# An eight-stage transformer kernel on one core: recurrence started on three takes, waits per norm chunk, a direct last reciprocal, bias rows laid out, a root table loaded at the start

## The chip, the cores and the metric

One core of one Trainium2 chip. The time is device microseconds of one launch; the kernel before has three timed runs, and one more run that the profiler recorded. Lines written as L12 are lines of the kernel before.

## The reference

The input x is one sequence of 2048 tokens of width 128, in f32. Eight blocks follow, each with its residual, `x = x + f(layernorm(x))`:

1. an RWKV-6 recurrence: projections r, k, v, w of token-mixed inputs, per head (16 of width 8) `s = exp(w)*s + k v^T`, output `r (s + exp(u+k) v^T)`, a norm per head, the gate r and an output matrix;
2. a mixture of 8 experts with the two best gates (hidden width 256);
3. causal attention with rotation, 16 heads of width 8;
4. the mixture of step 2 again, with the same weights;
5. full attention with one head of width 128;
6. a mixture of 8 experts that takes only two distinct sets of weights (expert 0, and a perturbed copy shared by the other seven), hidden width 512, with an inner norm that feeds its router;
7. causal attention with low-rank keys and values, 8 query heads, 2 key heads;
8. the mixture of step 6 again.

```
s = jnp.exp(w_t)[..., None] * s + k_t[..., :, None] * v_t[..., None, :]
...
h = (x - mu) * jax.lax.rsqrt(var + 1e-05) * ln_gamma + ln_beta
probs = jax.nn.softmax(logits, axis=-1)
out = jnp.einsum('bse,besh->bsh', probs, y)
```

## The kernel before

x (`X`), its norm (`H`) and the transposed norm (`HT`, features on partitions) stay in SBUF. The 2048 tokens are 16 tiles of 128, or NC = 4 chunks of 512 (TPC = 4 tiles each). Every stage is a class with one method per engine (`sync`, `gpsimd`, `tensor`, `scalar`, `vector`), and each engine runs the methods of all stages in their order, so its instructions run in exactly the order that the code writes. Semaphores alone hold the engines together; DMAs of the stages are issued from SP.

**LayerNorm** (L191 on). VectorE makes statistics, ScalarE takes the root of the variance (L298, or L249 for one chunk), VectorE takes the reciprocal (L280) and normalises (L283, L234), TensorE transposes a chunk into a PSUM bank (L242), and ScalarE copies it to `HT` (L259), which raises `ready` by one per chunk. A norm behind a mixture or the recurrence has chunks 0 to 2 done while the stage before it still runs; behind an attention all four are made at its start. The banks are 0 to 3. The next stage's TensorE waits for `all_ready`, all four chunks.

**Rwkv** (L708 on). For each chunk of 512 tokens ScalarE *takes* six results (`take`): k, w, r and v out of four PSUM banks, w scaled, and `ek = exp(u+k)`. VectorE then computes `rk = r*ek` (L838), and for each of 8 state columns j: the outer product `kvj` (L789) from TensorE's repeated values (`values`, L958), the recurrence as one scan (L844), and `rsj = r*state` (L861), which TensorE sums over j into bank 6 (L1008). TensorE sums rk over heads (L998) into bank 0, ahead of its loop over j, and VectorE multiplies that with v (`bonus`, L800) at j = 1. The next chunk's projections (L946, L947) are issued at j = 5. VectorE adds both parts at the chunk's end (`output`, L794), and TensorE centres the sum and takes its variance (L966, L971) at the start of the next chunk.

**Experts** (L1029 on). For each chunk and expert: `hidden` (L1065), gelu on ScalarE (L1118), `output`: a 3-row matmul that puts the bias rows in the bank (L1076, its moving operand the expert's row of 128 read four times through a step of 0), then L1083, and VectorE's gated addition to x (L1148). In the first chunk the router (L1191, then a chain of small VectorE operations from L1205) comes behind `hidden` of expert 1; in the two mixtures of the second kind the inner norm stands ahead of it.

**CausalHeads** (L1240 on), used twice, as `rope` and `latent`. A prologue projects `HT` (L1441, L1443), projects the values (L1449), splits the results in three bf16 parts and writes and rereads them through DRAM by SP. `make_plan` then writes out an order for scores, exponentials, weighted sums and a ring of small items in PSUM banks 5 to 7. For `latent` the sums of a chunk of queries are one item `total` (L1505); they are copied to SBUF (L1766), moved by a DMA into a 128x16 tile, inverted (L1705), moved back by a DMA, spread over the partitions by a matmul (item `sum`, L1498), multiplied with O (L1761), and multiplied with the output weights (item `out`, L1512; then L1772).

**FullHead** projects q, k, v (L1977, L1982), and then goes tile by tile. `Perturb` runs on GpSimd alongside stages 2 to 5 and delivers the second set of weights of stage 6; its bias rows are split by VectorE in eight small steps that end with L578.

## Time and profile before

| | |
|---|---|
| median of 3 runs | 1744.61 us (1743.3 to 1746.62) |
| the profiled execution | 1749.35 us |
| its span | 1747.3 us |
| mean granted TensorE clock in it | 0.935 of full |
| TensorE busy | 1561.8 us (89%) |
| VectorE busy | 1071.8 us (61%) |
| ScalarE busy | 793.4 us (45%) |
| GpSimd busy | 748.2 us (43%) |

All rows come from the one profiled execution, which took 4.7 us more than the median of the other runs. Starts are microseconds from the span's start. A group of matmuls in f32 counts each multiplication twice (two passes). A row's bracket names the idle time of its engine ahead of it and what ended it.

### The profile page before, as it was taken

To read this page: it belongs to the slowest core of one execution; us is meant where nothing else is said; L and a number is where in the kernel's file an instruction comes from. 1 tells how busy PE (TensorE), PEld (TensorE's weight loads), DVE (VectorE), ACT (ScalarE), POOL (GpSimd) and SP (SyncE) were. 2 spreads that over 40 slices of the span, in tenths; PEclk is the share of its full clock that TensorE was granted. 3 is DMA by queue.
4 is the path that set the end of the run, shared out by engine and by line. 5 is a ranking of instruction groups with operands and counts; after the bars stand their busy time and mean duration, and the time that the engine had idled before them with its cause. 6 is when DMAs were issued, how large, how long until landed. Compare 5 with 4: busy or idle time off the path is not lost.

```text
span 1747.3 us, 25466 instructions
## 1 busy us (share of the span) xinstructions
PE 1561.8 (89%) x8943; PEld 803.1 (46%) x8943; DVE 1071.8 (61%) x2338; ACT 793.4 (45%) x1037; POOL 748.2 (43%) x963
## 2 busy tenths in 40 slices
PE   5886999689999999999799979997978799999789
PEld 2433666323343333343266647775744343343256
DVE  5777433798788788786143333334348889885541
ACT  2231444615555555556534424445452334445442
POOL 1000663654635455463645546360002457777600
PEclk9998899859999999999889989998988899999879
DMA  5000000323002011000000000000034100000000
GB/s 154 0 1 1 1 1 1 121 54 56 2 2 56 2 28 30 2 2 3 1 1 1 1 1 0 0 0 1 1 99 131 40 24 2 2 1 2 1 7 19
DMA packets 41353, 37.18 MB, mean 21 GB/s; under 512 B 12404, under 2 KB 38493, under 8 KB 41117
## 3 DMA queue, kind: packets, MB, share of 16 engines
q1 hardware_dynamic: 38948, 28.61, 5.8%
q10 hardware_dynamic: 2136, 7.10, 2.1%
q8 instruction: 70, 1.15, 0.3%
q14 instruction: 39, 0.31, 0.1%
q0 software_dynamic: 160, 0.01, 0.0%
HBM read 26.09 MB, written 8.91 MB: 20 GB/s over the span
## 4 chain that ended last, share of the span: by engine, by line
PE 70%; DVE 13%; ACT 3%; issue 3%; DMA 1%; POOL 1%; SPq 1%; DVEq 0%; POOLq 0%; ACTq 0%
PE PS L1539 11%; PE PS L1083 10%; PE PS L1481 10%; PE PS L1558 10%; PE PS L1065 9%; PE PS L1993 3%; PE PS L2011 3%; DVE sb_rope_mp L1728 3%; DVE sb_latent_mp L1728 2%; PE PS L2005 1%; PE PS L1498 1%; PE PS L1076 1%; POOL sb_H L1649 1%; PE PS L1512 1%; PE PS L1191 1%
## 5 line engine op out<-in xcount | busy, mean ns | idle before, releaser
L1728 DVE TENSOR_REDUCE sb_rope_mp<-PS 128x1 f32<-128x512 f32 (+3 forms) x560 | 344.6, 668 | 68.7 <-PE PS L1485 31.9
L1600 ACT ACTIVATE sb_rope_PT<-PS 128x1024 f32<-128x1024 f32 (+3 forms) x320 | 273.4, 895 | 210.5 <-PE PS L1543 109.4
L1148 DVE SCALAR_TENSOR_TENSOR sb_X<-PS,sb_gates,sb_X 128x128 f32<-128x128 f32 x320 | 90.1, 344 | 225.7 <-PE PS L1083 225.3
L1481 PE MATMUL PS<-sb_rope_K,sb_rope_Q 96*128 96x512 bf16 (+3 forms) x640 | 213.6, 373 | 11.5 <-ACT sb_rope_V L1585 7.9
L643 POOL TENSOR_SCALAR sb_pbelow<-sb_pa,sb_ptrial 128x512 f32<-128x512 f32 x124 | 194.7, 1581 | 6.4
L1728 DVE TENSOR_REDUCE sb_latent_mp<-PS 128x1 f32<-128x512 f32 (+2 forms) x280 | 176.0, 668 | 26.8 <-PE PS L1481 15.8
L650 POOL TENSOR_TENSOR sb_pbelow<-sb_pbelow 128x1024 f32<-128x1024 f32 (+1 forms) x248 | 181.4, 731 | 19.6
L1065 PE MATMUL PS<-sb_HT,sb_w 128*128 128x512 f32 x384 | 182.7, 613 | 4.3 <-DVE sb_seed L578 1.9
L1539 PE MATMUL PS<-sb_rope_Q,sb_rope_K 99*128 99x512 bf16 (+3 forms) x640 | 180.2, 353 | 1.6 <-ACT sb_rope_PT L1600 0.9
L1558 PE MATMUL PS<-sb_rope_PT,sb_rope_V 128*9 128x512 f32 (+3 forms) x1280 | 149.8, 540 | 0.1
L1539 PE MATMUL PS<-sb_latent_Q,sb_latent_K 96*128 96x512 bf16 (+7 forms) x640 | 149.7, 353 | 0.0
L1118 ACT ACTIVATE sb_moe_hidden<-PS,sb_vec 128x512 f32<-128x512 f32 x128 | 86.7, 687 | 130.4 <-PE PS L1065 124.4
L1481 PEld LDWEIGHTS PS<-sb_rope_K,sb_rope_Q 96*128 96x128 bf16 x640 | 59.8, 100 | 167.8 <-issue 82.2
L1083 PE MATMUL PS<-sb_w0b,sb_moe_hidden 128*128 128x128 f32 x1024 | 133.7, 285 | 0.0
L1083 PEld LDWEIGHTS PS<-sb_w0b,sb_moe_hidden 128*128 128x128 f32 x1024 | 121.3, 194 | 14.7 <-issue 14.7
L1481 PE MATMUL PS<-sb_latent_K,sb_latent_Q 96*128 96x512 bf16 (+3 forms) x320 | 102.3, 369 | 12.7 <-DVE sb_latent_mp L1728 6.0
L1065 PEld LDWEIGHTS PS<-sb_HT,sb_w 128*128 128x128 f32 x384 | 70.8, 198 | 71.2 <-issue 66.7
L656 POOL TENSOR_TENSOR sb_ptot<-sb_ptot,sb_prank 128x8 f32<-128x8 f32 x31 | 6.2, 200 | 221.3 <-issue 221.3
L655 POOL PARTITION_ALL_REDUCE sb_ptot<-sb_pcnt x31 | 13.3, 427 | 185.3 <-issue 185.3
L1539 PEld LDWEIGHTS PS<-sb_rope_Q,sb_rope_K 99*128 99x128 bf16 x640 | 59.0, 99 | 69.5 <-issue 17.1
L1539 PEld LDWEIGHTS PS<-sb_latent_Q,sb_latent_K 99*128 99x128 bf16 (+1 forms) x640 | 57.1, 99 | 72.7 <-issue 17.0
L1543 PE MATMUL PS<-sb_mask_kq,sb_identb 128*128 128x128 bf16 x384 | 81.2, 226 | 0.0
(330 smaller groups left out, 2496.4 us busy)
## 6 DMA issues: line engine op xcount, KB each, us to landing
sb_latent_Q<-latent_parts SPq DMA_DIRECT2D x48, 128.0 KB, 2.7
sb_rope_Q<-rope_parts ACTq DMA_DIRECT2D x9, 384.0 KB
rope_parts<-sb_rope_parts SPq DMA_DIRECT2D x24, 128.0 KB, 2.4
latent_parts<-sb_latent_parts SPq DMA_DIRECT2D x12, 256.0 KB, 2.5
sb_rope_tab<-in_rotation SPq DMA_DIRECT2D x1, 2048.0 KB, 7.8
sb_rope_K<-rope_parts ACTq DMA_DIRECT2D x6, 256.0 KB
latent_parts<-sb_latent_parts SPq DMA_DIRECT2D x12, 128.0 KB, 2.5
sb_latent_K<-latent_parts SPq DMA_DIRECT2D x48, 32.0 KB, 2.2
```

What stands on the lines that cost most here:

```text
L643: ch.mark(g.tensor_scalar(self.below[:, w, s, :], self.a[:, w, :], tr[:, 2 * w + s:2 * w + s + 1], None, ALU.is_lt))
L650: ch(g.tensor_tensor(bl[:, :, 0:n], bl[:, :, 0:n], bl[:, :, n:2 * n], ALU.add))
L1065: pe.matmul(k.bank(b), self.w1(e, m), x, start=True, stop=True).then_inc(self.hid[b], 1)
L1083: ins = pe.matmul(k.PS[:, 4 + b, i * P:(i + 1) * P], self.g[:, b, m, i * P:(i + 1) * P], self.w2(e, m), start=False, stop=(m == M - 1), sk ...
L1118: s.activation(self.g[:, e % 2, m, :], k.bank(b), self.func, bias=self.b1(e, m)) \
L1148: ins = v.scalar_tensor_tensor(xi, k.PS[:, 4 + b:5 + b, i * P:(i + 1) * P], gate, xi, ALU.mult, ALU.add)
L1481: ins = pe.matmul(k.PS[:, bank, at:at + w], self.Q[0:self.rows, g % 2, j, 0, q0:q0 + P], self.K[0:self.rows, g % 2, j % self.kheads, 0, kc ...
L1539: ins = pe.matmul(k.PS[:, j, q0:CH], self.K[0:r, g % 2, j % self.kheads, m, kj * P:(kj + 1) * P], self.Q[0:r, g % 2, j, m, c * CH + q0:(c ...
L1543: ins = pe.matmul(k.PS[:, j, q0:q0 + P], k.identb[:, :], k.mask_kq[:, :], start=False, stop=True)
L1558: ins = pe.matmul(k.PS[32 * j:32 * j + self.vcols, 4, q0:CH], v, self.PT[u % self.B][:, j, q0:CH], start=(kj == 0), stop=(kj == last))
L1600: s.activation(self.PT[u % self.B][:, 2 * p:2 * p + 2, q0:CH], k.PS[:, 2 * p:2 * p + 2, q0:CH], ACT.Exp, scale=self.scale).then_inc(self.e ...
L1728: ins = v.tensor_reduce(self.mp[:, n % 2, kc, heads[0]:heads[-1] + 1, i], k.PS[:, bank, 0:len(heads) * w].rearrange("p (h k) -> p h k", h= ...
```

## The change

It has seven parts.

1. *Table at the start.* `Setup.scalar` takes the root of a column of constants, ahead of everything else on ScalarE; `sd` is overwritten by the first norm later.
2. *Three takes.* The order of the projections and takes is w, k, r, v (was k, w, r, v), w is scaled right behind the take of k, and VectorE starts a chunk's first outer product after three takes. The first `rsj` waits for the fourth, `rk` stands behind the outer product of j = 1 and waits for all six.
3. *Bonus two steps on.* TensorE's matmul on rk moves from the head of the chunk to behind the sum of j = 1, VectorE's `bonus` from j = 1 to j = 3.
4. *Waits per chunk.* TensorE waits for chunk c of the norm only where it projects chunk c, in the mixtures and in both causal stages; the router, the inner norm and the value projections wait for all. In the full attention the wait for all stays ahead of the first projection. Every norm but the first transposes into banks 4 to 7.
5. *Bias rows.* Per mixture a tile `seeds` holds the rows four times over, written by four DMAs from SP, which waits for the norm's statistics (and for the rows themselves); the moving operand of L1076 is then contiguous.
6. *Direct last reciprocal.* The last chunk of the last causal stage has an item `direct` in the place of `total`, both DMAs, the 128x16 reciprocal and `sum`: VectorE inverts each 128x128 quarter of the PSUM bank in place and multiplies O with it, and `out` starts on each quarter as it is ready.
7. One new semaphore per mixture, and the counts and waits that go with these parts.

```
--- before.py
+++ after.py
     def scalar(self, s):
         s.wait_ge(self.zeroed, self.n_zeroed)
+        s.activation(self.k.ln_mem.sd[:, 0:1], self.k.eps[:, :], ACT.Sqrt).then_inc(self.pool, 1)
+        s.wait_ge(self.pool, 1)
...
-            v.wait_ge(self.taken, (c + 1) * self.TAKEN)
-            if c:
-                v.wait_ge(self.bonus, c)
-            v.tensor_tensor(self.rk[:, :], self.r[:, c % 2, :], self.ek[:, :], ALU.mult).then_inc(self.rk_ready, 1)
+            v.wait_ge(self.taken, c * self.TAKEN + 3)
             outer(c, 0)
...
                 if j == 1:
+                    v.wait_ge(self.taken, (c + 1) * self.TAKEN)
+                    if c:
+                        v.wait_ge(self.bonus, c)
+                    v.tensor_tensor(self.rk[:, :], self.r[:, c % 2, :], self.ek[:, :], ALU.mult) \
+                        .then_inc(self.rk_ready, 1)
+                if j == 3:
                     bonus(c)
...
+                if j == 0:
+                    v.wait_ge(self.taken, c * self.TAKEN + 4)
...
-            plain = [(self.kk, 1, ACT.Copy), (self.w, 3, ACT.Sigmoid), (self.r, 0, ACT.Sigmoid), (self.v, 2, ACT.Copy)]
+            plain = [(self.w, 3, ACT.Sigmoid), (self.kk, 1, ACT.Copy), (self.r, 0, ACT.Sigmoid), (self.v, 2, ACT.Copy)]
...
-            s.wait_ge(self.taken, c * self.TAKEN + 2)
-            s.activation(self.w[:, p, :], self.w[:, p, :], ACT.Copy, scale=float(np.exp(-1e-4))).then_inc(self.taken, 1)
+                if i == 1:
+                    s.wait_ge(self.taken, c * self.TAKEN + 1)
+                    s.activation(self.w[:, p, :], self.w[:, p, :], ACT.Copy, scale=float(np.exp(-1e-4))) \
+                        .then_inc(self.taken, 1)
...
-            for n, bank in ((1, 1), (2, 3), (0, 0)):
+            for n, bank in ((2, 3), (1, 1), (0, 0)):
...
-            pe.wait_ge(self.rk_ready, c + 1)
-            pe.matmul(k.bank(0), k.group_sum, self.rk[:, :], start=True, stop=True).then_inc(self.bonus, 1)
             for j in range(8):
...
+                if j == 1:
+                    pe.wait_ge(self.rk_ready, c + 1)
+                    pe.matmul(k.bank(0), k.group_sum, self.rk[:, :], start=True, stop=True).then_inc(self.bonus, 1)
...
+        self.seeds = self.k.sb(self.name + "_seeds", [3, self.E, TPC, P], BF16, ctx)
+
+    def sync(self, sp):
+        for sem, val in self.needs:
+            sp.wait_ge(sem, val)
+        sp.wait_ge(self.ln.mem.moments, self.ln.all_ready)
+        for i in range(TPC):
+            sp.dma_start(self.seeds[:, :, i, :], self.seed[:, :, :]).then_inc(self.seeded, 16)
...
-        pe.wait_ge(self.ln.ready, self.ln.all_ready)
         def turn(c, first):
+            pe.wait_ge(self.ln.ready, self.ln.chunk_ready(c))
...
-                pe.matmul(k.bank(4 + b), k.onesb[0:3, :],
-                          self.seed[:, e:e + 1, :].broadcast_to([3, TPC, P]), start=True, stop=False,
+                if c == 0 and e == 0:
+                    pe.wait_ge(self.seeded, self.seeded_at)
+                pe.matmul(k.bank(4 + b), k.onesb[0:3, :], self.seeds[:, e, :, :], start=True, stop=False,
...
-            if first:
+            if first and self.between:
+                pe.wait_ge(self.ln.ready, self.ln.all_ready)
...
+                if n == len(self.order) - 1:
+                    steps[end + 2] += [("direct", g, c), ("out", g, c)]
+                    continue
...
-        pe.wait_ge(self.ln.ready, self.ln.all_ready)
         for c in range(NC):
+            pe.wait_ge(self.ln.ready, self.ln.chunk_ready(c))
...
                 pe.wait_ge(self.filled, self.use + 1)
+                pe.wait_ge(self.ln.ready, self.ln.all_ready)
...
-        pe.wait_ge(self.normed, n + 1)
         for i in range(TPC):
+            pe.wait_ge(self.normed, n + 1 + (i if ("direct", g, c) in self.ring_items() else 0))
...
+        elif kind == "direct":
+            n = self.chunk(*item[1:])
+            v.wait_ge(self.moved, n + 1)
+            for i in range(TPC):
+                tile = slice(i * P, (i + 1) * P)
+                ch(v.reciprocal(k.PS[:, bank, tile], k.PS[:, bank, tile]))
+                ch(v.tensor_tensor(self.On[:, n % 2, tile], self.O[:, n % 2, tile], k.PS[:, bank, tile], ALU.mult))
+                v.sem_inc(self.normed, 1)
+            v.sem_inc(free, 1)
...
-            ln = LayerNorm(k, k.X, k.H, k.HT, x_ready)
+            ln = LayerNorm(k, k.X, k.H, k.HT, x_ready, banks=(4, 5, 6, 7) if len(stages) > 1 else (0, 1, 2, 3))
```

The change moves instructions in the recurrence. On VectorE, at the start of the first chunk, these rows stood before (rw_rk is r times ek, rw_kvj the outer product, the operation on rw_state the scan, rw_rsj the state times r, rw_o the bonus):

```order
L838 TENSOR_TENSOR sb_rw_rk<-sb_rw_r,sb_rw_ek 128x512 [waits rwkv_taken]
L789 TENSOR_TENSOR sb_rw_kvj<-sb_rw_k,PS 128x512 [waits rwkv_vrep0]
L844 SCALAR_TENSOR_TENSOR sb_rw_state<-sb_rw_w,sb_rw_state,sb_rw_kvj 128x512 [waits rwkv_kv0,rwkv_steps]
L789 TENSOR_TENSOR sb_rw_kvj<-sb_rw_k,PS 128x512 [waits rwkv_vrep1]
L861 TENSOR_TENSOR sb_rw_rsj<-sb_rw_r,sb_rw_state 128x512 [waits rwkv_kv_used0]
L844 SCALAR_TENSOR_TENSOR sb_rw_state<-sb_rw_w,sb_rw_state,sb_rw_kvj 128x512 [waits rwkv_kv1]
L789 TENSOR_TENSOR sb_rw_kvj<-sb_rw_k,PS 128x512 [waits rwkv_kv_used0,rwkv_vrep0]
L800 TENSOR_TENSOR sb_rw_o<-PS,sb_rw_v 128x512 [waits rwkv_bonus]
L861 TENSOR_TENSOR sb_rw_rsj<-sb_rw_r,sb_rw_state 128x512 [waits rwkv_kv_used1]
```

Now, in the same place:

```order
L793 TENSOR_TENSOR sb_rw_kvj<-sb_rw_k,PS 128x512 [waits rwkv_vrep0,rwkv_taken]
L845 SCALAR_TENSOR_TENSOR sb_rw_state<-sb_rw_w,sb_rw_state,sb_rw_kvj 128x512 [waits rwkv_kv0,rwkv_steps]
L793 TENSOR_TENSOR sb_rw_kvj<-sb_rw_k,PS 128x512 [waits rwkv_vrep1]
L870 TENSOR_TENSOR sb_rw_rsj<-sb_rw_r,sb_rw_state 128x512 [waits rwkv_taken,rwkv_kv_used0]
L845 SCALAR_TENSOR_TENSOR sb_rw_state<-sb_rw_w,sb_rw_state,sb_rw_kvj 128x512 [waits rwkv_kv1]
L793 TENSOR_TENSOR sb_rw_kvj<-sb_rw_k,PS 128x512 [waits rwkv_kv_used0,rwkv_vrep0]
L853 TENSOR_TENSOR sb_rw_rk<-sb_rw_r,sb_rw_ek 128x512 [waits rwkv_taken]
L870 TENSOR_TENSOR sb_rw_rsj<-sb_rw_r,sb_rw_state 128x512 [waits rwkv_kv_used1]
```

The product rk went from ahead of the first outer product to behind the third, into the place where the bonus stood; the bonus itself is two steps further on.

On TensorE, in the same chunk, before (rw_mixv to wvrep is the repeated value, rw_rk the head sum of the bonus, rw_rsj the output sum):

```order
L958 MATMUL PS<-sb_rw_mixv,sb_wvrep 128x512 [waits setup_ready]
L958 MATMUL PS<-sb_rw_mixv,sb_wvrep 128x512
L998 MATMUL PS<-sb_rw_rk,sb_cst 128x512 [waits rwkv_rk_ready]
L958 MATMUL PS<-sb_rw_mixv,sb_wvrep 128x512 [waits rwkv_kv0]
L1008 MATMUL PS<-sb_rw_rsj,sb_cst 128x512 [waits rwkv_rs0]
```

and now:

```order
L969 MATMUL PS<-sb_rw_mixv,sb_wvrep 128x512 [waits setup_ready]
L969 MATMUL PS<-sb_rw_mixv,sb_wvrep 128x512
L969 MATMUL PS<-sb_rw_mixv,sb_wvrep 128x512 [waits rwkv_kv0]
L1017 MATMUL PS<-sb_rw_rsj,sb_cst 128x512 [waits rwkv_rs0]
L969 MATMUL PS<-sb_rw_mixv,sb_wvrep 128x512 [waits rwkv_kv1]
L1017 MATMUL PS<-sb_rw_rsj,sb_cst 128x512 [waits rwkv_rs1]
L1021 MATMUL PS<-sb_rw_rk,sb_cst 128x512 [waits rwkv_rk_ready]
```

The third repeated value no longer stands behind the head sum. The same moves are made in all four chunks.

## Rows read from the trace of the kernel before

**Rows 1.** The profile's page: busy time by engine, and the chain's shares.

```profile
PE 1561.8 (89%) x8943; PEld 803.1 (46%) x8943; DVE 1071.8 (61%) x2338; ACT 793.4 (45%) x1037; POOL 748.2 (43%) x963
...
PE 70%; DVE 13%; ACT 3%; issue 3%; DMA 1%; POOL 1%; SPq 1%; DVEq 0%; POOLq 0%; ACTq 0%
```

**Rows 2.** Timeline of the start: start us, duration us, engine, line, instruction, count.

```profile
11.85 1.28 ACT L298 ACT_TABLE_LOAD   x1 [11.85 <-DVE sb_mv L277]
...
20.78 2.04 PE L946 MATMUL PS<-sb_HT,sb_wmix 128*128 128x512 f32 x2 [1.58 <-DVE sb_wvrep L459]
```

**Rows 3.** Timeline, first chunk of the recurrence.

```profile
29.90 1.88 PE L958 MATMUL PS<-sb_rw_mixv,sb_wvrep 128*128 128x512 f32 x4
...
33.24 0.90 DVE L838 TENSOR_TENSOR sb_rw_rk<-sb_rw_r,sb_rw_ek 128x512 f32<-128x512 f32 x1 [9.35 <-ACT sb_rw_ek L898]
34.07 0.67 DVE L789 TENSOR_TENSOR sb_rw_kvj<-sb_rw_k,PS 128x512 f32<-128x512 f32 x1
```

**Rows 4.** Timeline, second, third and fourth chunk of the recurrence.

```profile
62.33 0.68 DVE L838 TENSOR_TENSOR sb_rw_rk<-sb_rw_r,sb_rw_ek 128x512 f32<-128x512 f32 x1
62.93 0.68 DVE L789 TENSOR_TENSOR sb_rw_kvj<-sb_rw_k,PS 128x512 f32<-128x512 f32 x1
...
68.05 2.06 PE L998 MATMUL PS<-sb_rw_rk,sb_cst 128*128 128x512 f32 x2
...
69.89 1.71 PE L958 MATMUL PS<-sb_rw_mixv,sb_wvrep 128*128 128x512 f32 x2
...
71.64 0.69 DVE L789 TENSOR_TENSOR sb_rw_kvj<-sb_rw_k,PS 128x512 f32<-128x512 f32 x1 [4.26 <-PE PS L958]
...
101.30 1.40 PE L998 MATMUL PS<-sb_rw_rk,sb_cst 128*128 128x512 f32 x2
...
104.45 0.69 DVE L789 TENSOR_TENSOR sb_rw_kvj<-sb_rw_k,PS 128x512 f32<-128x512 f32 x1 [1.37 <-PE PS L958]
...
134.12 1.10 PE L998 MATMUL PS<-sb_rw_rk,sb_cst 128*128 128x512 f32 x2
...
136.12 0.69 DVE L789 TENSOR_TENSOR sb_rw_kvj<-sb_rw_k,PS 128x512 f32<-128x512 f32 x1 [0.23 <-PE PS L958]
```

**Rows 5.** Timeline, where stages 2, 3 and 6 begin.

```profile
170.28 1.11 PE L242 MATMUL PS<-sb_cst,sb_H 128*128 128x128 f32 x4 [3.90 <-DVE sb_H L234]
...
172.13 6.13 PE L1065 MATMUL PS<-sb_HT,sb_w 128*128 128x512 f32 x8 [0.73 <-issue]
...
322.17 0.69 DVE L1676 TENSOR_TENSOR sb_rope_x<-PS,sb_rope_tab 128x512 f32<-128x512 f32 x1 [3.63 <-DMA sb_rope_tab<-in_rotation]
...
1204.92 8.60 PE L1065 MATMUL PS<-sb_HT,sb_w 128*128 128x512 f32 x16 [1.92 <-DVE sb_seed L578]
```

**Rows 6.** Stretch of 1 us: busy per engine, then PEclk, DMA share, GB/s.

```profile
172.00:173.00 1.00, 0.87 (x1) 0.50 (x2) 0.00 (x0) 0.03 (x1) 0.57 (x6) 0.50 0.00 0
```

**Rows 7.** Timeline of TensorE, full clock, in stage 2 and in stage 3.

```profile
229.22 0.38 PE L1076 MATMUL PS<-sb_seed,sb_onesb 3*128 3x512 bf16 x1
229.53 2.05 PE L1083 MATMUL PS<-sb_w0b,sb_moe_hidden 128*128 128x128 f32 x16
...
564.74 0.38 PE L1481 MATMUL PS<-sb_rope_K,sb_rope_Q 96*128 96x512 bf16 x1
565.05 1.05 PE L1558 MATMUL PS<-sb_rope_PT,sb_rope_V 128*9 128x512 f32 x8
```

**Rows 8.** Timeline, end of stage 7, with one reciprocal and one product from elsewhere.

```profile
75.53 0.55 DVE L807 RECIPROCAL sb_rw_sd<-sb_rw_sd 128x64 f32<-128x64 f32 x1
...
182.78 0.29 DVE L1205 TENSOR_TENSOR sb_rt_p<-PS,sb_bg 128x128 f32<-128x128 f32 x1 [12.55 <-PE PS L1191]
...
1647.03 1.93 PE L1505 MATMUL PS<-sb_H,sb_cst 128*32 128x512 f32 x8 [3.54 <-POOL sb_H L1649]
...
1651.66 0.25 DVE L1705 RECIPROCAL sb_latent_inv<-sb_latent_sums 128x16 f32<-128x16 f32 x1 [1.95 <-DMA sb_latent_sums<-sb_latent_x]
...
1658.92 0.69 DVE L1772 TENSOR_TENSOR sb_X<-sb_X,PS 128x512 f32<-128x512 f32 x1 [2.29 <-PE PS L1512]
```

9 lines of the change are left out of this document (7 added, 2 removed).

## The prediction, made before the changed kernel was run

> **What bounds the kernel now.** I read the page first: TensorE is busy 89% of the span and holds 70% of the chain that ended last, VectorE 13% [rows 1]. So an edit pays only where TensorE stands idle, or where VectorE holds the chain: the start, the head of each chunk of the recurrence, the seams between stages and the tail of stage 7. I then read the timeline at each of those places, TensorE and VectorE side by side; in every row the bracket says how long the engine had stood still and who ended that. A row without a bracket follows its forerunner directly. Last I looked at the granted clock where TensorE had just been idle, because a matmul there takes about twice its time [rows 4, 6].
>
> The sum is made against the profiled execution, 1749.35 us, 4.7 above the median of the runs. I take off the gains there and then those 4.7.
>
> **Table at the start.** ScalarE loads the root table for 1.28 us after VectorE's statistics are there [rows 2]; the normalised x waits for that root, and TensorE's first projection waits on VectorE behind it, with 1.58 idle [rows 2]. The new root on a constant column makes the load before the statistics, while ScalarE waits anyway. Gain 1.28 at most, 0 at least if the chain through L459 were set by other VectorE work; I take **-1.3**, since the load stands between two links of that chain.
>
> **Three takes, first chunk.** VectorE began with rk at 33.24, released by ek, the last of the takes after 9.35 idle, and the outer product followed at 34.07 [rows 3]. The outer product now needs k, w and the first repeated value. The four passes of the two repeated values start at 29.90 and take 1.88, 0.47 each [rows 3], so the first value is there at about 30.9. That is 3.1 earlier. The product rk isn't gone: it moves behind the third outer product and costs its slot there, 0.60 from its start to the next one's [rows 4]. Something of the rest is lost where the first rsj waits for the fourth take. 3.1 - 0.6 = 2.5 is the upper bound; a lower one is 1.9, if rsj waits 0.6; I take **-2.2**. The table of the sigmoid is also loaded behind the first projection now and not ahead; that lies beside the four passes of k's projection, and nobody waits for it.
>
> **The other three chunks.** The head sum L998 stood ahead of the third repeated value on TensorE, and VectorE waited for that value: 4.26, 1.37 and 0.23 in chunks two to four [rows 4]. In chunk two L998 takes 2.06 and its successor starts 1.84 later; in chunk three it takes 1.40, in chunk four 1.10 [rows 4]. It leaves this place (its new one, behind the sum of j = 1, is where TensorE waits for VectorE), and the wait shrinks by its slot. VectorE pays 0.60 for rk behind the outer product, as it did ahead of the first, where it was hidden in the wait. So: chunk two -1.84 + 0.6 = -1.2; chunk three about -1.2 + 0.6 = -0.6; in chunk four only 0.23 of wait and the freed 0.6 ahead can be won, some -0.2. Together **-2.0**, from 0 (the projections of the next chunk simply absorb it) to -3. The bonus two steps later has the same length in the same stream: 0. What is late next in these places is the repeated value itself, 1.71 for its two passes at the low clock [rows 4].
>
> **Waits per chunk.** In stage 2 the last transposes end, TensorE stands 0.73 for ScalarE's copy, and the first `hidden` begins [rows 5]. Chunk 0 has long been copied, so the new wait is met: TensorE can go on behind its transposes, at most 0.95 early, which is the copy and the hand-over (170.28 + 1.11 to 172.13 is 0.74; the ends of matmuls are modelled, and a wait that doesn't exist saves its own latency too, about 0.2). But the granted clock stands at 0.50 there [rows 6], the 1.2 GHz level, after TensorE had waited 3.90 for VectorE [rows 5]. If the clock rises at the same instant as before and not earlier, the early microsecond is worked at half speed and half of the gain is gone: 0.45. I take 0.7, and four such seams (stages 2, 4, 7 and 8): **-2.8**. In stage 3 the same wait goes, but VectorE's first product waits until 322.17 for the DMA that brings the rotation table [rows 5], which nobody moves: 0 to -0.9, I take **-0.4**. In stage 6 TensorE waits for L578 on VectorE, 1.92 [rows 5], and not for the norm: 0. In the full attention the wait for all stays: 0. The router and inner norm still wait for all, but they come two `hidden` later, when all chunks are there. Other banks for the transposes take a possible wait for `hidden`'s banks away: 0, since the first group of the next stage uses banks that are free. Together **-3.2**, bounds 0 and -5.
>
> **Bias rows laid out.** The matmul with the repeated row holds TensorE for 0.31 from its start to the next one's, its record is 0.38. A bf16 matmul over 512 columns with a contiguous operand, in the scores of stage 3, shows 0.31 and 0.38 as well ahead of an f32 matmul [rows 7]. So the step of 0 costs nothing that could be won: **0**. The rows' DMAs (four per mixture, on SP) start at the norm's statistics and are wanted behind the first two `hidden`, at least 10 us later: hidden. If that cover were gone, TensorE would stand by what is missing of a transfer.
> The Trainium skill, "TensorE: Matmul & The Clock Gate", section Back-to-back issue gap, gives about 216 ns for an isolated warm matmul of N=512; by that the slot of 0.31 would hide 0.1 of something, and with 80 such matmuls the sum would have 7.5 more to win. The neighbouring row speaks against it.
>
> **Direct last reciprocal.** Now, from the sums' matmul on: start 1647.03, 1.93 long, copy, DMA out, 0.25 of reciprocal at 1651.66, DMA back, `sum`, product, `out`; VectorE's addition starts at 1658.92 after 2.29 for L1512 [rows 8]. In its place come four times a reciprocal of 128x128 and a product. No row has this reciprocal. The nearest are 128x64 with 0.55 and 128x16 with 0.25 [rows 8], both in SBUF: a slope of 0.30/48 = 6.25 ns per element of a partition gives 0.95. Lower bound 0.55 (no longer than half of it), upper bound 2 (PSUM in place at twice the slope); I take 0.95, along the line through both rows. The product takes 0.29 [rows 8], the hand-over some 0.06: 1.3 per quarter, 5.2 for four, from 1649.0 to 1654.2. TensorE's `out` on quarters one to three runs underneath; the last needs about 0.5. VectorE then adds at 1654.7, not 1658.92: **-4.2**. With 0.55 it would be -5.8, with 2 a quarter it is 0.
> By the Trainium skill, "VectorE: DVE Perf Modes", section First, the fixed hardware budget, a reciprocal is divided iteratively with a repeat count of 8; at the 0.96 GHz of its Specifications that is 8.3 ns per element, by my estimate 1.2 a quarter and -3.2 for the part. The step between the two rows is somewhat smaller than this rule's.
>
> **Sum.** -1.3 - 2.2 - 2.0 - 3.2 - 4.2 = -12.9: 1736.4 for a profiled execution like the one shown, **1731.7** for the median.
>
> **The rivals.**
> *Other waits take the place of the norm's.* For: stage 3 does it already, by the table's DMA, and the clock is at its low level at the seam [rows 5, 6]. Against: in stages 2, 4, 7 and 8 nothing else is late. Then -3.2 goes: 1734.9. Chance 0.14.
> *The reciprocal in PSUM is slow.* For: no row has one from PSUM. Against: the product with a PSUM operand takes 0.29 for 128 columns, nothing unusual [rows 8]. At 2 a quarter the part gives 0: 1735.9. From there on it would lose. Chance 0.08.
> *The repeated row is what costs the bias matmul.* For: 0.38 is long for 512 columns at full clock. Against: the contiguous row of the same group [rows 7]. Worth 0.1 x 80 = 7.5 to 8: 1724. Chance 0.07.
> *The clock is lost in the recurrence: slower.* TensorE there runs at both levels; a pass costs 1.71 / 2 = 0.86 at the low one and 1.88 / 4 = 0.47 at the full one [rows 3, 4]. The head sum filled TensorE for 1 to 2 us at each chunk's start. With it gone from there, and VectorE's stream longer by rk at j = 1, TensorE has a longer idle stretch, and the granted clock may fall and stay low over the 16 passes of the next chunk's projections: 16 x 0.39 = 6.2 at each of three seams. One seam gives 1737.9; two 1744.1, no change; all three 1750.3, slower. It decides when the third falls. Against it: chunk two runs low already at the head without its projections having been lost, and the passes only change place. One seam 0.02 (it counts to faster), two 0.02, three 0.03.
> *It doesn't do what it says,* since each removed wait was met before: the starts stay where they are, 1744.6. The brackets speak against it. Chance 0.02.
>
> **How the numbers follow.** The forecast has the rest, 0.64. Its own bounds: the direct part from 0.55 to 1.3 a reciprocal, +1.4 and -1.6; recurrence +2 and -1; seams +3.2 and -1.8; table +1.3; these don't fall together, and each low-clock stretch may shift, by some 1.7 us, as the 2.06 against 1.10 of the head sum shows. The runs themselves lie within 3.3. I give **1725.5 to 1738.0**: it reaches from just above the bias-row rival to one seam of lost clock, and leaves out some 0.15 to 0.2. About 3.5 us, 0.2%, is what a measurement of this kernel can tell from no change. Faster: the forecast, the first three rivals, one seam lost: 0.95, less 0.02 for a forecast that meets several bounds at once: 0.93. Same, two seams, a change that does nothing, and nothing more: 0.04. Slower: 0.03.
>
> **What would show it.** Right: the load of the root table before the statistics; the first outer product near 29.7, released by the repeated value; no head sum between the second and third repeated value; in stage 2 the first `hidden` within about 0.2 of the transposes; four reciprocals of about 0.95 in the last chunk, and VectorE's last addition 4 us sooner; the bias matmul's slot still at 0.31. Wrong: reciprocals of 2 us or more, a granted clock of 0.5 over the projections inside the recurrence, or TensorE waiting for the rows' DMAs in a first chunk.

## The result, and the profile after

The changed kernel takes 1731.08 us (median of 6 runs, 1722.39 to 1733.3) against 1745.47 of the kernel before (6 runs, 1743.3 to 1746.86): ratio 0.9913, with a 95% interval of 0.9897 to 0.993, so 14.4 us faster. 1731.7 was forecast. Lines are those of the changed kernel from here on, unless it says "before".

The profiled execution, though, took 1722.39 us: 27 below that of before, not 14. A single profile of this kernel stands several us off its median, as the runs below show. The page's first part and the chain's shares answer to [rows 1]:

```profile
PE 1546.3 (90%) x8941; PEld 799.8 (46%) x8941; DVE 1076.7 (63%) x2343; ACT 793.2 (46%) x1038; POOL 748.2 (43%) x963
...
PE 71%; DVE 13%; ACT 3%; issue 3%; POOL 1%; DMA 1%; SPq 1%; DVEq 0%; POOLq 0%; ACTq 0%
```

TensorE is busy 15.5 us less with the same matmuls but one (the last chunk's `sum`, two passes, 2.05 us before). The rest is the clock: a wait taken away can't shorten a matmul. To see where, I cut both traces at the first matmul of each part: the first `hidden` of stages 2, 4, 6 and 8, the first projection and the first score of stages 3 and 7. The view gives busy time per engine in each stretch, then the granted clock, the DMA share and GB/s. Before:

```profile
0.00:172.10 172.10, 124.75 (x367) 58.75 (x367) 124.35 (x262) 45.84 (x71) 6.22 (x21) 0.95 0.14 39
172.10:317.90 145.80, 140.40 (x720) 91.93 (x720) 55.17 (x205) 59.85 (x83) 83.72 (x137) 0.94 0.02 6
317.90:350.70 32.80, 21.57 (x64) 10.29 (x64) 26.86 (x40) 26.76 (x28) 18.27 (x27) 0.86 0.48 145
350.70:880.20 529.50, 490.31 (x3265) 188.61 (x3265) 397.95 (x755) 285.46 (x343) 270.74 (x453) 0.93 0.10 19
880.20:1204.90 324.70, 301.93 (x1680) 209.03 (x1680) 120.48 (x334) 137.04 (x206) 154.44 (x247) 0.96 0.00 1
1204.90:1285.40 80.50, 73.62 (x392) 52.36 (x392) 29.75 (x141) 41.85 (x58) 0.00 (x0) 0.92 0.00 1
1285.40:1309.50 24.10, 16.60 (x57) 8.63 (x58) 14.81 (x24) 16.06 (x32) 0.00 (x0) 0.85 0.57 172
1309.50:1670.00 360.50, 321.31 (x2025) 132.24 (x2025) 283.97 (x499) 150.69 (x175) 214.77 (x80) 0.92 0.09 25
```

After:

```profile
0.00:162.20 162.20, 119.84 (x368) 58.11 (x369) 124.33 (x262) 45.10 (x71) 7.04 (x21) 0.95 0.14 42
162.20:305.40 143.20, 137.62 (x721) 89.87 (x721) 57.78 (x205) 59.63 (x83) 81.08 (x134) 0.96 0.02 5
305.40:337.50 32.10, 21.34 (x66) 10.46 (x64) 26.30 (x41) 27.26 (x29) 17.49 (x26) 0.87 0.51 152
337.50:858.10 520.60, 486.02 (x3265) 187.95 (x3265) 396.04 (x754) 284.80 (x342) 268.25 (x447) 0.94 0.09 20
858.10:1182.60 324.50, 302.40 (x1681) 209.14 (x1680) 120.21 (x333) 137.81 (x207) 160.02 (x258) 0.96 0.00 1
1182.60:1262.30 79.70, 73.54 (x392) 52.53 (x393) 29.76 (x141) 41.29 (x56) 0.00 (x0) 0.93 0.00 1
1262.30:1285.10 22.80, 15.34 (x58) 8.21 (x56) 14.75 (x24) 16.70 (x33) 0.00 (x0) 0.87 0.59 181
1285.10:1643.30 358.20, 318.90 (x2023) 132.29 (x2024) 288.54 (x501) 150.11 (x174) 214.28 (x80) 0.93 0.09 25
```

The first stretch gives 9.9, the last one shown 2.3, and those with the seams around stages 2, 3 and 7 together 5 to 6; behind it, stage 8 takes 77.3 in both. The fourth, 8.9, is the main part of stage 3, in which the change touches nothing but the seam at its end, where stage 4 begins.

At the chosen places, the timeline (start us, duration us, engine, line, instruction) answers to [rows 2] and [rows 3] like this:

```profile
11.86 0.31 ACT L300 ACTIVATE sb_sd<-sb_mv,sb_eps 128x16 f32<-128x16 f32 x1 [9.63 <-DVE sb_mv L279]
...
19.49 1.10 PE L957 MATMUL PS<-sb_HT,sb_wmix 128*128 128x512 f32 x2 [1.30 <-DVE sb_wvrep L463]
...
25.57 3.00 PE L969 MATMUL PS<-sb_rw_mixv,sb_wvrep 128*128 128x512 f32 x6
...
26.70 0.69 DVE L793 TENSOR_TENSOR sb_rw_kvj<-sb_rw_k,PS 128x512 f32<-128x512 f32 x1 [4.11 <-PE PS L969]
```

The root follows the statistics with no load between, the first projection comes 1.3 earlier, and the outer product is released by TensorE and no longer by ek. But the projection takes 1.10 for two passes and not 2.04: here the clock had come up before it, in the trace of before only at 26.9. So the outer product starts 7.4 earlier, where 1.3 + 3.1 had been worked out.

Stage 2's seam and VectorE's first product of stage 3 answer to [rows 5], stage 7's tail to [rows 8]:

```profile
161.26 1.11 PE L244 MATMUL PS<-sb_cst,sb_H 128*128 128x128 f32 x4 [3.89 <-DVE sb_H L236]
162.17 5.13 PE L1087 MATMUL PS<-sb_HT,sb_w 128*128 128x512 f32 x8
162.41 0.60 ACT L261 ACTIVATE sb_HT<-PS 128x512 f32<-128x512 f32 x1 [2.57 <-PE PS L244]
...
310.11 0.69 DVE L1704 TENSOR_TENSOR sb_rope_x<-PS,sb_rope_tab 128x512 f32<-128x512 f32 x1 [3.17 <-DMA sb_rope_tab<-in_rotation]
```

```profile
1626.59 0.97 DVE L1797 RECIPROCAL PS<-PS 128x128 f32<-128x128 f32 x1 [2.67 <-PE PS L1533]
1627.59 0.29 DVE L1798 TENSOR_TENSOR sb_latent_On<-sb_latent_O,PS 128x128 f32<-128x128 f32 x1
1628.02 0.97 DVE L1797 RECIPROCAL PS<-PS 128x128 f32<-128x128 f32 x1
...
1633.12 0.69 DVE L1809 TENSOR_TENSOR sb_X<-sb_X,PS 128x512 f32<-128x512 f32 x1 [0.95 <-PE PS L1540]
```

The first `hidden` starts 0.91 behind the transposes' start, before 1.85, while ScalarE still copies the last chunk; the table's DMA still ends VectorE's wait; a reciprocal takes 0.97 and a quarter 1.43. At stage 4 the same wait of 0.73 is gone, first before, then after:

```profile
880.18 4.10 PE L1065 MATMUL PS<-sb_HT,sb_w 128*128 128x512 f32 x5 [0.73 <-issue]
```

```profile
857.19 1.12 PE L244 MATMUL PS<-sb_cst,sb_H 128*128 128x128 f32 x4 [0.46 <-DVE sb_H L285]
858.10 4.47 PE L1087 MATMUL PS<-sb_HT,sb_w 128*128 128x512 f32 x6
```

The bias matmul with the contiguous row keeps its slot of 0.31 (221.31 to 221.62) and its record [rows 7]:

```profile
221.31 0.39 PE L1100 MATMUL PS<-sb_moe_seeds,sb_onesb 3*128 3x512 bf16 x1
221.62 1.05 PE L1106 MATMUL PS<-sb_w0b,sb_moe_hidden 128*128 128x128 f32 x7
```

### The profile page after: what moved, and what is told of

It reads as the page before. It is cut to its first block, busy times and chain, and to the rows that moved or that the text cites. A ratio compares the mean times of both kernels' runs of the same rounds, so it can differ in the third digit from the quotient of the medians.

```text
span 1720.6 us, 25513 instructions
## 1 busy us (share of the span) xinstructions
PE 1546.3 (90%) x8941; PEld 799.8 (46%) x8941; DVE 1076.7 (63%) x2343; ACT 793.2 (46%) x1038; POOL 748.2 (43%) x963
## 4 chain that ended last, share of the span: by engine, by line
PE 71%; DVE 13%; ACT 3%; issue 3%; POOL 1%; DMA 1%; SPq 1%; DVEq 0%; POOLq 0%; ACTq 0%
PE PS L1567 11%; PE PS L1106 11%; PE PS L1509 10%; PE PS L1586 10%; PE PS L1087 10%; PE PS L2031 3%; PE PS L2049 3%; DVE sb_rope_mp L1756 3%; DVE sb_latent_mp L1756 2%; PE PS L2043 1%; PE PS L1100 1%; POOL sb_H L1677 1%; PE PS L1526 1%; PE PS L1540 1%; PE PS L1513 1%
## 5 line engine op out<-in xcount | busy, mean ns | idle before, releaser
L1509 PE MATMUL PS<-sb_latent_K,sb_latent_Q 96*128 96x512 bf16 (+3 forms) x320 | 101.4, 367 | 14.8 <-DVE sb_latent_mp L1756 8.3
L1513 PE MATMUL PS<-sb_mask_qk,sb_identb 128*128 128x128 bf16 x384 | 81.0, 236 | 0.0
```

The costliest lines, as they stand in the source:

```text
L1509: ins = pe.matmul(k.PS[:, bank, at:at + w], self.Q[0:self.rows, g % 2, j, 0, q0:q0 + P], self.K[0:self.rows, g % 2, j % self.kheads, 0, kc ...
L1513: ins = pe.matmul(k.PS[:, bank, at + w - P:at + w], k.identb[:, :], k.mask_qk[:, :], start=False, stop=True)
```

## The experiments

Twelve kernels ran, each beside runs of the kernel before on the same chip. Those 88 runs of before have a mean of 1746.5, a median of 1745.9, and lie between 1734.97 and 1760.84. Each run has its span and its mean granted clock, and with the two levels that gives the time at the lower one, 2 x (1 - clock) x span: 230 us on average for before. Among these 88 runs of one program, a run with 1 us more at the low level is 0.41 us longer (correlation 0.84). Most of the spread goes with that. For kernels that ran 12 times the mean has a standard error of 0.9 to 1.7 us, for 6 to 8 times 1.2 to 3.1, and a +- is one such error; I use medians and intervals as measured, and means where parts are added up.

### One part alone, on the kernel before

Part 1 alone:

```
         s.wait_ge(self.zeroed, self.n_zeroed)
+        s.activation(self.k.ln_mem.sd[:, 0:1], self.k.eps[:, :], ACT.Sqrt).then_inc(self.pool, 1)
+        s.wait_ge(self.pool, 1)
```

> The kernel before with part 1 alone (the root of a constant column at the start). Theory of waits: the load of 1.28 goes from between the statistics and the root, and nothing else, 1.3 us faster than before. Theory of the clock: the profile of the changed kernel has its first repeated value at 25.57 where before has it at 29.90, 4.3 earlier, because its first projections run 1.02 per pair of passes and not 2.04; if the earlier load is what brings the clock up sooner, this kernel alone is 3 to 4.5 us faster and its first projection takes 1.1 and not 2.04. If the moment at which the clock rises is a matter of chance, the runs of this kernel spread over some 3 us and the median stands near -1.3 to -2.5.

Measured: median 1742.52, ratio 0.9978 (0.9956 to 1.0), mean -3.6 against all runs of before. In the profile the first repeated value comes at 27.2 and the first `hidden` at 169.9; in three traces with an unchanged start they come at 28.4 to 29.9 and 171.1 to 172.1. The projection took 2.05 at first and full clock came at 22.9; the unchanged starts have it between 24 and 27. So 1.3 is the load. The clock's rise differs by up to 3 us between unchanged starts, and one trace at 22.9 doesn't tell whether the earlier load moves it.

Parts 2 and 3 alone:

```
-            v.wait_ge(self.taken, (c + 1) * self.TAKEN)
...
-            v.tensor_tensor(self.rk[:, :], self.r[:, c % 2, :], self.ek[:, :], ALU.mult).then_inc(self.rk_ready, 1)
+            v.wait_ge(self.taken, c * self.TAKEN + 3)
             outer(c, 0)
```

> The kernel before with part 2 and 3 alone (three takes, rk behind the outer product of j = 1, bonus at j = 3). Theory of waits, as predicted: -4.2 (first chunk -2.2, chunks two to four -2.0). Theory that the prediction undersized it: the span from the first repeated value to the first hidden of stage 2 was 142.2 in the profile of before and is 136.6 in that of the changed kernel, so -5.6. Clock theory: the difference beyond 4.2 comes from low stretches at another place, and then this run shows pairs of passes of 1.7 to 2.06 at other places than before and a median anywhere from -2 to -8.

Measured: median 1738.35, ratio 0.9955 (0.9936 to 0.9973), mean -7.6. The first `hidden` comes at 167.8, 3.8 below the mean 171.6 of the three unchanged ones: the prediction's 4.2. For the rest of the 7.6, 3.8, there is the time at the low level, 221 us a run against 230, which at 0.41 is 3.5; that is a match of two numbers and not shown to be the cause.

Part 4 alone:

```
-        pe.wait_ge(self.ln.ready, self.ln.all_ready)
         def turn(c, first):
+            pe.wait_ge(self.ln.ready, self.ln.chunk_ready(c))
```

> The kernel before with part 4 alone (waits per chunk, banks 4 to 7). Theory of waits: -3.2 (0.7 at stages 2, 4, 7 and 8, 0.4 at stage 3). Rival, other waits take the place: 0. Clock theory: the 27 us between the two profiles are only 14 between the medians, and 9 of them lie in stage 3's main part, where the low stretch shrank from 44 to 31 us; if the earlier start by the copy's wait moves such stretches, this kernel's runs spread by 5 us or more and its median can lie 5 or more below before.

Measured: median 1743.68, ratio 0.9966 (0.9942 to 0.999), mean -5.7. The runs fall apart in five at 1730 to 1737 and seven at 1744 to 1749, with 217 us at the low level. By stages: stage 7 starts 0.8 earlier behind stage 6 and its prologue takes 22.8 and not 24.1. The rows of stage 7's prologue show why, before and then after: four passes in 3.78, and in 2.88.

```profile
1285.41 3.78 PE L1441 MATMUL PS<-sb_HT,sb_wc 128*128 128x512 f32 x4 [0.69 <-ACT sb_HT L259]
```

```profile
1262.34 2.88 PE L1468 MATMUL PS<-sb_HT,sb_wc 128*128 128x512 f32 x4
1265.05 1.02 PE L1468 MATMUL PS<-sb_HT,sb_wkv 128*128 128x512 f32 x2
```

TensorE reached full clock sooner, where the prediction feared that the clock would stay put. Stage 7's main part took 1.1 of it back. Together 1.1 for the two seams of stages 7 and 8, and 1.2 up to stage 3's first projection. At stage 4, 0.94 comes on top: from the start of the last four transposes to the first `hidden` it is 1.85 at stages 2 and 4 in all six traces without the part and 0.91 in all eight with it.

Part 6 alone:

```
+                if n == len(self.order) - 1:
+                    steps[end + 2] += [("direct", g, c), ("out", g, c)]
+                    continue
```

> The kernel before with part 6 alone (direct last reciprocal). Predicted -4.2 at 0.95 per reciprocal and 1.3 per quarter. The changed kernel's profile shows 0.97 per reciprocal and 1.43 per quarter, and from the sums' matmul to the last addition 8.5 instead of 11.9: by that -3.4. Nothing ahead of stage 7's tail may differ; if the median is off by more than 1.5 from -3.4, the runs' own spread is larger than their median tells.

Measured: median 1742.78, ratio 0.9973 (0.9951 to 0.9996), mean -4.5. Stage 7's main part takes 357.0 and not 360.5: -3.5, as the rows of the tail give.

Part 5 alone:

```
-                          self.seed[:, e:e + 1, :].broadcast_to([3, TPC, P]), start=True, stop=False,
+                pe.matmul(k.bank(4 + b), k.onesb[0:3, :], self.seeds[:, e, :, :], start=True, stop=False,
```

> The kernel before with part 5 alone (bias rows laid out four times by DMAs). Theory as predicted: 0, and the bias matmul's slot still 0.31. Rival, the repeated row is what costs: 80 times 0.1, -7.5 to -8, with a slot of 0.22; the changed kernel's trace has records of 0.38 for it, as before, so this rival is already weak. What is still open is a cost: the four DMAs per mixture and SP's wait; if they delayed anything, this kernel would be slower than before by 1 us or more and the first bias matmul of a mixture would stand behind a DMA.

Measured: median 1743.93 against 1744.78 in the same rounds, ratio 0.9999 (0.9976 to 1.0022). Its first `hidden` is at 171.5, and the slot stays 0.31 to 0.32 (239.61 to 239.93). No gain, no cost.

### The changed kernel again

> The changed kernel once more, on the same chip and beside the same runs of before. The six first runs lie at 1722 to 1725 (two) and 1730 to 1733 (four). Theory of waits: median 13 to 15 below before. Sum of the single parts, by their means over 12 runs against before: table 3.9, takes 7.9, waits 6.0, direct 4.8, together 22.6; if the parts simply add, this kernel stands 20 to 24 below before. Clock theory: two groups of runs some 7 us apart, by whether stage 3 begins with a low stretch of 44 or of 31 us, and a median that follows from how many fall in each.

Measured: 1729.86 (1718.87 to 1737.18, 6 runs), ratio 0.9896 (0.9856 to 0.9935). Over both sets, 12 runs, the mean is 1729.3, 17.1 +- 1.8 below before, the median 1731.1. The five parts alone sum to 3.6 + 7.6 + 5.7 + 4.5 + 1.3 = 22.7 +- 3.9: more than 17.1, though not by enough to call it shown. The six new runs fall apart in three at 1718.9 to 1724.6 and three at 1735.1 to 1737.2, as the clock theory had it, though further. This second profile is the best control there is, the same program at 1736.0 us:

```profile
0.00:162.60 162.60, 120.41 (x367) 58.55 (x368) 124.41 (x262) 45.10 (x71) 8.52 (x21) 0.95 0.14 42
162.60:305.70 143.10, 137.28 (x722) 89.83 (x721) 57.54 (x205) 59.52 (x83) 80.19 (x133) 0.98 0.02 5
305.70:339.10 33.40, 19.95 (x67) 9.76 (x66) 27.50 (x41) 27.36 (x29) 17.37 (x26) 0.91 0.50 152
339.10:871.50 532.40, 492.13 (x3264) 190.06 (x3265) 398.75 (x754) 284.99 (x342) 275.50 (x458) 0.93 0.09 19
```

Stages 1 and 2 repeat within 0.5, stage 3's main part takes 532.4 instead of 520.6, with 75 us at the low level instead of 60. In the thirteen traces other than this one, with and without the parts, it lies anywhere between 518.8 and 529.5. So the 8.9 between the first two profiles there prove nothing about the change.

### One part undone, on the changed kernel

> The changed kernel with parts 2 and 3 undone. Theory of waits (prediction): 4.2 slower than the changed kernel, and in the profile the first hidden of stage 2 comes 4 later than at 162.2 to 162.6. Sum of the run means of the single part: 7.5 slower, of which 3.7 by less time at the low clock (221 against 230 us a run, at the 0.41 us per us that the runs of before show). Theory of an interaction: the recurrence gained 8.3 in the changed kernel against 6.3 for its three parts alone; if the parts need each other (the table at the start and the order of the takes), the first hidden comes 6 later.

Measured: median 1736.61, ratio to before 0.9951 (0.9929 to 0.9974); its mean is 7.8 +- 2.2 above the changed kernel's. The first `hidden` is at 168.7; in the four traces that keep all of the change's parts and add nothing to the recurrence it is at 162.2 to 164.1, so 4.6 to 6.5 later, where waits alone would give 4 and the theory of an interaction 6. In these traces (all but `table_split`) and in this one the first projection ran at full clock, so the first chunk can be compared. Its sum is added here, and then in the changed kernel, at:

```profile
57.20 0.69 DVE L798 TENSOR_TENSOR sb_rw_o<-sb_rw_o,PS 128x512 f32<-128x512 f32 x1 [6.02 <-PE PS L1012]
```

```profile
55.00 0.69 DVE L798 TENSOR_TENSOR sb_rw_o<-sb_rw_o,PS 128x512 f32<-128x512 f32 x1 [6.01 <-PE PS L1017]
```

That is 2.2, the prediction's figure for the first chunk.

> The changed kernel with part 4 undone. By the stages of the profiles so far, the part gives 0.8 at the first hidden of stage 2, 1.2 at the start of stage 3, 0.8 at the start of stage 7 and 1.3 in its prologue, and takes 1.1 back in stage 7's main part; so 3 slower than the changed kernel. Clock theory: in stage 3's main part kernels with the part show 519 to 532 us and kernels without it 520 to 530; if the part makes the short low stretch more frequent, this kernel is 5 to 6 slower than the changed one and has 10 us more at the low level per run.

Measured: median 1737.41, ratio 0.9948 (0.9927 to 0.9969), mean 9.0 +- 2.0 above the changed kernel's, with 222 us at the low level against its 212. Stage 2 to stage 3 takes 144.8 and not 143.2, stage 7's prologue 24.1. And the first `hidden` comes at 167.4, of which 0.94 is the seam, though the recurrence is the changed kernel's. The stretch from 58 to 135 in this kernel, and then in the changed one:

```profile
58.00:135.00 77.00, 65.74 (x160) 29.85 (x161) 59.73 (x96) 20.47 (x27) 0.00 (x0) 0.87 0.00 0
```

```profile
58.00:135.00 77.00, 63.49 (x167) 27.85 (x167) 63.43 (x102) 21.47 (x30) 0.00 (x0) 0.96 0.00 0
```

A clock of 0.87 against 0.96 is 20 us at the low level against 6, and TensorE got 6 or 7 matmuls less done in more busy time. It isn't the missing part that does this: `warm_prologue`, which has it, has the same low stretch of 10.3 us from 58.

So both parts are worth 6 to 9 us in whole runs, alone or undone. In rows of their own stages the takes show 4 to 6 of that and the waits about 4.6.

### What stands behind the table's DMA

The rotation table in two DMAs, chunk 0's columns first:

```
+            sp.dma_start(self.tab[:, :, 0:CH], tab[:, :, 0:CH]).then_inc(self.table0, 16)
+            sp.dma_start(self.tab[:, :, CH:], tab[:, :, CH:]).then_inc(self.table, 16)
```

> The changed kernel, with the rotation table of stage 3 loaded by two DMAs, the first with the columns of chunk 0 alone. Theory (the table's DMA ate the seam of stage 3): VectorE's first product no longer waits for the DMA but for TensorE, some 1.5 to 2.7 us earlier, and the first score comes 1 to 2.7 earlier; the median 1 to 2.7 below the changed kernel. Rival, the prologue is bound by ScalarE and VectorE further on or by the rereads through DRAM: the first product is earlier, the first score is not, 0.

Measured: median 1729.25 (8 runs), ratio 0.9913 (0.9883 to 0.9943). VectorE's first product is now released by TensorE:

```profile
310.86 0.69 DVE L1707 TENSOR_TENSOR sb_rope_x<-PS,sb_rope_tab 128x512 f32<-128x512 f32 x1 [1.65 <-PE PS L1471]
```

It comes 3.2 behind stage 3's first projection (before 4.2, changed 4.7), and the prologue takes 31.0 instead of 32.1 and 33.4. So the DMA did eat part of the seam of stage 3, and 1 to 2 us were to be had. Whole runs don't show them: the mean is 1.5 +- 2.7 above the changed kernel's.

### Keeping the clock up

```
+        pe.wait_ge(self.values, self.use * NC + 2)
+        for n in range(5):
+            pe.matmul(k.bank(5), k.ident, k.HT[:, 1:1 + CH], start=True, stop=True)
```

> The changed kernel with five matmuls of 128x512 in f32 that nobody reads, in the idle time of TensorE (6.3 and 5.8 us) ahead of the first score of both causal stages. This computes nothing that the output uses. Clock theory (the low stretch at the beginning of stage 3, 31 or 44 us long, comes from TensorE's idle time ahead of it and costs half its length where TensorE holds the chain): the stretch is shorter or gone and the time is 5 to 15 us below the changed kernel, with less spread between runs. Rival, the low stretch comes from the scores themselves, whose matmuls of 96 rows run with short breaks, and not from the idle time: the stretch stays, 0, or up to 2 slower if the five matmuls run at the low level and delay the first score.

Measured: median 1728.29 (6 runs, 1721.33 to 1732.61), ratio 0.9902; the mean is 1.5 +- 2.3 below the changed kernel's, though its runs have only 198 us at the low level, not 212. In the changed kernel's profile the clock is low from 1.6 ahead of stage 3's first score to 5.2 behind it, and from 8.6 to 39.3; here from 1.4 to 38.9. That is 37.5 us at the low level in either. So the idle time ahead, cut from 6.3 to 2.3, isn't what makes the stretch; the rival, that it comes from the scores, is what is left, on one trace. In the changed kernel's profile TensorE is busy 28.3 of 30 us in that stretch, at a clock of 0.53:

```profile
348.40:378.40 30.00, 28.30 (x94) 9.05 (x93) 27.80 (x52) 3.84 (x4) 15.56 (x26) 0.53 0.10 21
```

By the two profiles what is saved at the low level lies elsewhere: against the changed kernel's first, 1.3 us less ahead of stage 3's scores, 3.5 ahead of stage 7's, 9 in stages 4 to 6, where nothing was edited, and 7 more in stage 1. Why 14 us less at the low level gave no more than 1.5 +- 2.3 stays open.

### Two further versions

Chunks two to four's rk and `difference` on GpSimd, on top of the two edits above, and one wait less per quarter of the reciprocal:

```
+    def gpsimd(self, g):
+        for c in range(NC):
+            if c:
+                g.wait_ge(self.taken, (c + 1) * self.TAKEN)
+                g.wait_ge(self.bonus, c)
+                g.tensor_tensor(self.rk[:, :], self.r[:, c % 2, :], self.ek[:, :], ALU.mult).then_inc(self.rk_ready, 1)
```

> The changed kernel with four further edits: the rotation table in two DMAs; five unread matmuls ahead of the first scores of both causal stages; the products rk of chunks two to four and the differences of chunks two to four on GpSimd instead of VectorE; and one semaphore wait less per quarter of the direct reciprocal. Theory (VectorE's stream of 2.4 us per state column holds the recurrence): 0.6 for each of six products taken off it, 3.6, if GpSimd's products don't slow VectorE down; the table 1.6; the tail 0.6; the unread matmuls 0 to 2. Together 5 to 8 below the changed kernel. Rival: TensorE or the shared access of GpSimd and VectorE holds the chunk, and the recurrence gains nothing or loses: then 2 below.

Measured: median 1730.24 (6 runs, 1728.81 to 1736.54), ratio 0.991 (0.9879 to 0.9941): no better than the changed kernel. Yet the first `hidden` stands at 158.1, and a quarter of the last reciprocal takes 1.20 instead of 1.43 (from the sums' matmul to the last addition 7.8 instead of 8.5), so the wait left out had cost 0.23 a quarter. The gain went behind stage 1: stage 2 to stage 3 takes 147.9 instead of 143.2, stage 6 82.5 instead of 79.7, stage 7's prologue 24.3 instead of 22.8. Of the first of these, 1.7 is in the timeline ahead of stage 3: four normalised tiles take 3.17, while GpSimd runs stage 6's preparation; in the other thirteen traces they take 1.2 to 1.9. For the rest, more of stages 2 and 6 lies at the low level (14.8 and 17.6 us against 10.1 and 11.4).

```profile
301.90 3.17 DVE L236 TENSOR_SCALAR sb_H<-sb_X,sb_mv,sb_rstd 128x128 f32<-128x128 f32 x4
...
302.65 3.69 POOL L654 TENSOR_TENSOR sb_pbelow<-sb_pbelow 128x1024 f32<-128x1024 f32 x2
```

GpSimd's loop there runs at its own pace from the end of stage 1 on, so an earlier stage 2 meets it at another point. And VectorE's copy of the state took 0.92 at chunks two and three, not 0.17, while GpSimd ran `difference`.

The last version drops the unread matmuls and adds one wait on GpSimd ahead of rk, `g.wait_ge(self.kv[0], c * 4 + 1)`.

> The last kernel without the unread matmuls, and with GpSimd's products held back until VectorE has made a chunk's first outer product. In all_and_more the recurrence was 4.3 shorter than in the changed kernel (first hidden of stage 2 at 158.1 against 162.2 to 162.6), though VectorE's copy of the state took 0.92 instead of 0.17 at chunks two and three, while GpSimd ran its difference; behind it 3.4 were lost again: a norm ahead of stage 3 whose four tiles took 3.2 instead of 1.5 while GpSimd ran stage 6's preparation, and low stretches at other places in stages 2, 6 and 7. Theory of contention: the copies are back at 0.17, the first hidden comes at 156 to 157.5. Theory of chance for what follows: the norm ahead of stage 3 and the low stretches fall as they do in the changed kernel's profiles, and the median is 5 to 8 below the changed kernel's 1730 to 1731, so 1722 to 1726. Rival, the rest of the kernel gives each earlier start back: median at 1728 to 1731 whatever the recurrence gains.

Measured: median 1728.81 (6 runs, 1721.12 to 1738.16), ratio 0.9898 (0.985 to 0.9947): inside the changed kernel's range again. The copies are back:

```profile
L840 DVE COPY sb_rw_state<-sb_rw_state x4: 168/169/174, 22.5 to 120.6; 128x8 f32<-128x8 f32 x4
```

But the first `hidden` comes at 161.6 and not at 156 to 157.5. The contention has only moved, as the start of chunk two shows:

```profile
56.88 2.28 POOL L892 TENSOR_TENSOR sb_rw_rk<-sb_rw_r,sb_rw_ek 128x512 f32<-128x512 f32 x1 [14.89 <-DVE sb_rw_kvj L796]
...
58.60 1.11 DVE L869 TENSOR_TENSOR sb_rw_rsj<-sb_rw_r,sb_rw_state 128x512 f32<-128x512 f32 x1
59.63 2.05 DVE L848 TENSOR_TENSOR_SCAN sb_rw_state<-sb_rw_w,sb_rw_state,sb_rw_kvj 128x512 f32<-128x512 f32 x1
```

GpSimd's product took 2.28 instead of 1.26. Beside it VectorE's rsj took 1.11 and not 0.68, and beside GpSimd's `difference` behind it a scan took 2.05 and not 1.28. Either happened three times: 3.6 us on VectorE, where in all_and_more two copies and one scan had cost 2.3. Besides, this trace has three low stretches between 60 and 130, all_and_more had none; what those cost I can't say. No version is shown to beat the changed kernel.

## Why the prediction was right

**The sum.** 12.9 was forecast; 14.4 is the difference of the medians, 17.1 +- 1.8 that of the means over all runs. The waits went where the prediction said, so it is right in mechanism, and somewhat low. That the median met 1731.7 within 0.6 is luck: the same kernel's runs lie between 1718.9 and 1737.2, and terms that were too small (the waits) and too large (the reciprocal) stand beside a gain by the clock that wasn't in it. One slip is in the chances: the rivals add up to 0.38, so the forecast had 0.62 and not 0.64.

**Table at the start, -1.3.** The load lies before the statistics, and the first projection comes 1.3 earlier in all traces with the part. Right in size. In whole runs alone -3.6 +- 1.3, which leaves room for a sooner rise of the clock that the term didn't have. In eight traces of the changed kernel and its variants the clock first comes up at 16.5 to 18.5, ahead of the first projection, and in seven it stays; of the six traces of before and of single parts only `direct_alone` has such a rise, and there it falls again. No run shows which edit does it.

**First chunk, -2.2.** The outer product is released by the repeated value, as forecast. The chunk's sum is added at 55.0 in both traces of the changed kernel, against 60.0 to 61.7 in those with an unchanged start, mean 60.7; with the table's 1.3 the forecast was -3.5, measured -5.7. The term itself is sized right: 2.2 between `takes_undone` and the changed kernel, both with the early clock, and 2.6 for the takes alone. The other 2.2 is the clock: durations at the low level (2.04, 1.91 for two passes) had been carried over as they stood, and in the changed kernel those passes mostly ran at full clock.

**Other chunks, -2.0.** VectorE's waits behind the moved head sum answer to [rows 4]:

```profile
62.44 0.69 DVE L793 TENSOR_TENSOR sb_rw_kvj<-sb_rw_k,PS 128x512 f32<-128x512 f32 x1 [2.32 <-PE PS L969]
63.04 0.69 DVE L853 TENSOR_TENSOR sb_rw_rk<-sb_rw_r,sb_rw_ek 128x512 f32<-128x512 f32 x1
...
126.91 0.69 DVE L793 TENSOR_TENSOR sb_rw_kvj<-sb_rw_k,PS 128x512 f32<-128x512 f32 x1 [1.19 <-PE PS L969]
```

4.26 became 2.32, which is 1.94 where 1.84 was read from L998; 1.37 vanished; 0.23 became 1.19, since a low stretch (124.3 to 127.7) fell on that value. The chunks took 33.8, 31.9 and 26.2 instead of 36.3, 32.1 and 25.6 on average: -2.6, -0.2, +0.6, together -2.2. The sum is met, its parts only within what one low stretch moves; in `warm_prologue` and `waits_undone`, with 10.3 us at the low level from 58, the second chunk took 36.7 and 36.6.

**Waits per chunk, -3.2.** Measured about 4.6, so this term was sized too small. The seams of stages 2 and 4 gave 0.94 each, where 0.7 had been taken; stages 7 and 8 gave 1.1 together; and from the first `hidden` of stage 2 to stage 3's first score it is 175.4 to 176.5 in five traces, against 176.7 to 178.6 without the part, 1.6 less on average, where 0.4 had been taken. In stage 3, VectorE's first product comes 4.7 behind the first projection on average, 4.4 without the part: some 0.3 went behind the table's DMA, which is within the scatter of either group. Stage 6 gained nothing, as its wait for L582 says. The half that I had taken off for the clock wasn't lost in stage 7: the clock rose sooner. The rival that other waits take the place is out: the transposes are followed by `hidden` at once in all eight traces, and undone, the part costs 9 +- 2.

**Bias rows, 0.** Right, by slot, record and run. The rival is out. So what the Trainium skill gives in "TensorE: Matmul & The Clock Gate", section Back-to-back issue gap, as the gap of an isolated warm matmul of 512 columns, 216 ns, is not what these slots of 0.31 show, and the operand's step of 0 isn't the reason.

**Direct reciprocal, -4.2.** Measured -3.4 to -3.5. The reciprocal was 0.97 for 0.95; the error is in the hand-over, 0.17 per quarter for 0.06 (1.43 - 0.97 - 0.29), and in the last `out`, 0.8 for 0.5. With one wait less per quarter the slot is 1.20. By the Trainium skill's repeat count of 8 ("VectorE: DVE Perf Modes", First, the fixed hardware budget) I had estimated 1.2 for a reciprocal; the line through the two rows of before was the better guide, and holds from PSUM too. That the estimate's -3.2 for the part lies nearer to what was measured is chance, since the hand-over made up for it. The rival of a slow reciprocal (2 us for one) is out by the same row.

**The slower rival,** low clock over the next chunk's projections, didn't come: the busy time of TensorE in stage 1 fell from 124.8 to 119.8. Low stretches do fall into the recurrence, but with and without the change, at the ends of chunks and elsewhere; `all_and_more` alone had none there.

**What the prediction missed** is that the time at the low level as such falls, 230 to 212 us a run. At 0.41 that answers to 7 of the 17 us, of which the forecast had only the part at the seams. Added up by rows, its terms come to 13.7 (1.3, 2.2, 2.2, 4.6 and 3.4), and the early rise of the clock to 2.2 more. It is a reckoning, not a separation, and why there is less low time stays open: shorter waits and less low time go together in these parts. The one kernel that took low time alone, `warm_prologue`, speaks for caution: 14 us less would be 5.7 at 0.41 and gave 1.5 +- 2.3.
